# Tokens sorted by expert through DRAM: a mixture-of-experts stage moved from each batch to one pass over blocks of 128 slots at the end

## The reference

```python
xf = x.reshape(-1, Hd)
logits = xf @ Wg + bg
gates = jax.nn.softmax(logits, axis=-1)
idx = jnp.argmax(gates, axis=-1)
h = jax.nn.gelu(jnp.einsum('th,ehi->tei', xf, W1) + b1, approximate=False)
y = jnp.einsum('tei,eih->teh', h, W2) + b2
out = jnp.take_along_axis(y, idx[:, None, None], axis=1)[:, 0, :]
```

## Time and profile before

| | |
|---|---|
| time, median of 3 runs | 2138.87 us (2138.83 to 2142.31) |
| profiled execution, span | 2139.7 us |
| PE busy | 1961.1 us, 92% |
| DVE busy | 1713.5 us, 80% |
| ACT busy | 1318.5 us, 62% |
| POOL busy | 260.0 us, 12% |
| chain that ended last | PE 62%, DVE 27%, ACT 5%, DMA 3% |
| granted PE clock, 40 slices | 8 tenths in the first, 9 or more in the others |

### The profile page before, as it was taken

The page is one execution under the profiler, slowest core; times in us unless marked ns, Lnnn a source line. Parts: engine busy times, 40 slices in busy tenths (PEclk is TensorE's granted clock), DMA queues, the critical chain, the costliest instruction groups (busy, mean ns, idle before and its releaser), DMA issues.

```text
span 2139.7 us, 42900 instructions
## 1 busy us (share of the span) xinstructions
PE 1961.1 (92%) x17874; PEld 1108.8 (52%) x17874; DVE 1713.5 (80%) x2676; ACT 1318.5 (62%) x1957; POOL 260.0 (12%) x280
## 2 busy tenths in 40 slices
PE   4999988899999998889999998898999999889898
PEld 2677742424667773232566776333265777533235
DVE  8888878795878877699588887869878888786956
ACT  5666647386366655748546664565944666455682
POOL 1000001350000001035000000103500000011430
PEclk8999999999999999999999999999999999999999
DMA  6366700030055561012006665002001666300200
GB/s 275 75 127 129 142 32 13 10 113 11 21 103 129 126 120 34 6 32 91 11 21 126 126 127 124 12 2 102 22 11 44 133 123 130 94 13 9 94 2 11
DMA packets 424210, 156.39 MB, mean 73 GB/s; under 512 B 405928, under 2 KB 416560, under 8 KB 423120
## 3 DMA queue, kind: packets, MB, share of 16 engines
q1 hardware_dynamic: 423440, 151.54, 30.0%
q0 software_dynamic: 576, 2.10, 0.3%
HBM read 43.43 MB, written 2.16 MB: 21 GB/s over the span
## 4 chain that ended last, share of the span: by engine, by line
PE 62%; DVE 27%; ACT 5%; DMA 3%; issue 3%; POOL 0%; POOLq 0%; DVEq 0%; ACTq 0%; SPq 0%
DVE nmx L2052 14%; PE ps L655 11%; PE ps L657 11%; PE ps L656 11%; PE ps L1033 6%; PE ps L823 4%; PE ps L817 3%; PE ps L818 3%; PE ps L1019 3%; DMA arena<-arena 2%; PE ps L983 1%; DVE st L1691 1%; DVE arena L1862 1%; PE ps L1043 1%; PE ps L1100 1%
## 5 line engine op out<-in xcount | busy, mean ns | idle before, releaser
L2052 DVE TENSOR_REDUCE nmx<-ps 128x2 f32<-128x1024 f32 x384 | 444.7, 1218 | 15.2 <-PE ps L983 13.6
L1557 ACT ACTIVATE arena<-ps 128x512 f32<-128x512 f32 x768 | 406.3, 600 | 50.8 <-PE ps L1019 45.9
L655 PE MATMUL ps<-arena 128*128 128x512 f16 (+1 forms) x784 | 266.6, 340 | 1.3 <-DVE arena L1783 1.1
L657 PE MATMUL ps<-arena 128*128 128x512 f16 (+1 forms) x784 | 266.5, 340 | 0.0
L656 PE MATMUL ps<-arena 128*128 128x512 f16 (+1 forms) x784 | 266.5, 340 | 0.0
L1849 DVE TENSOR_SCALAR_CACHE_REDUCE ps<-ps 128x1536 f32<-128x1536 f32 x128 | 225.7, 1763 | 40.5 <-PE ps L657 39.8
L1033 PE MATMUL ps<-arena 128*17 128x256 f32 x3072 | 240.4, 389 | 0.0
L1862 DVE SCALAR_TENSOR_TENSOR arena<-arena,rs 128x1536 f16<-128x1536 f32 x128 | 231.6, 1810 | 4.2 <-ACT arena L1447 4.2
L1447 ACT ACTIVATE arena<-arena,rs 128x1536 f16<-128x1536 f32 x128 | 200.8, 1569 | 42.9 <-DVE rs L1855 42.9
L1440 ACT ACTIVATE arena<-ps,nm 128x1536 f32<-128x1536 f32 x128 | 197.1, 1540 | 10.3 <-DVE ps L1849 10.3
L817 PE MATMUL ps<-arena 128*128 128x128 f16 x1536 | 185.3, 219 | 1.6 <-DMA arena<-arena 1.6
(11 more groups left out here) (286 smaller groups left out, 3732.9 us busy)
## 6 DMA issues: line engine op xcount, KB each, us to landing
arena<-in_experts SPq DMA_DIRECT2D x4, 3840.0 KB, 11.5
arena<-in_weights SPq DMA_DIRECT2D x8, 929.0 KB, 19.1
arena<-arena SPq DMA_DIRECT2D x72, 64.0 KB, 2.1
arena<-in_ctx SPq DMA_DIRECT2D x4, 1024.0 KB, 5.3
arena<-arena SPq DMA_TRANSPOSE x256, 3.2
arena<-in_ctx_t SPq DMA_DIRECT2D x4, 1024.0 KB, 4.9
arena<-arena SPq DMA_DIRECT2D x72, 32.0 KB, 1.9
y<-in_x POOLq DMA_DIRECT2D x4, 512.0 KB, 4.2
```

Source lines behind the costliest of these rows:

```text
L655: mm(out_, lh, rh, start=(k == 0), stop=False)
L657: last = mm(out_, ll, rh, start=False, stop=(k == n - 1))
L1557: A(pr_[:, n % RING, :], ps[:, 4 + n % 3, :], ACT.Exp).then_inc(b_exp.sem, 1)
L2052: V.tensor_reduce(nmx[:, g_ % 2, ch, :, pp, i], ps[:, 2 * (z % 2):2 * (z % 2) + 2, :], AX.X, ALU.max, negate=True)\
```

## The change

The experts leave the batch loop. In every batch the normalised rows z (as fp16 halves, 512 values), the row of x after cross attention (256 values) and the token's number are collected in one SBUF tile `zx`, 520 words (2080 bytes) for each token. The logits are computed from DMA transposes of z, and the choice as before. A matmul with a triangular matrix of ones counts how many tokens before this one chose the same expert, and a running count `held` for each expert continues over the batches; together they give each token a slot. Expert e's slots begin at row e x 2432 of a DRAM tensor `zx_d`. Four indirect DMAs for each batch, 128 rows each, write the rows to their slots. In the last batch eight more DMAs write filler rows behind each expert's slots so far (7 x 640 and 896 rows, 11.2 MB).

At the end `block_tables` works out which 23 blocks of 128 slots exist (16 for 2048 tokens and at most 7 for experts' last blocks that are partly filled). The number of blocks is fixed at 23. For each block SP reads the block's row address into a register, loads z by a DMA transpose and x by a plain DMA into one of 6 buffers; PE reads the expert's address into a register and does 12 matmuls of 128 columns and 8 of 256 (the bias b2 comes in as two of them); ACT does two Gelus of 128 columns; DVE splits and adds; POOL scatters the 128 rows to the output by an indirect DMA, where filler slots have a row number beyond the bound and are skipped. The experts' weights are loaded and split once, in the last batch.

At a batch boundary `routed(b)` gives way to `next_window(b + 1)`, which does in a row what had been laid between the experts. `next_stats`, `next_moments` and `next_rows` move further forward, into cross attention; they read the next batch's x from a buffer of its own, `xn`, loaded by SP in the place of the experts' weights. The choice for batch b - 1 (`route_logits`, `route_choice`, `route_ranks`, `route_slots`) is done inside `windowed(b)`. ACT loads the Gelu table once, and the Exp table no longer at the start of `windowed`. The matmuls of `keep_warm` in `routed` are gone.

```diff
+            def keep_rows(b):
+
+                sp.wait_ge(lx_added.sem, lx_added.at(b, 2 * NT))
+                if b < B - 1:
+                    sp.wait_ge(b_mm.sem, b_mm.at(b, 192))
+                sp.dma_start(zx[:, :, D:2 * D], x[:]).then_inc(xc_in.sem, 16)
+
+            def transpose_rows(b):
+
+                sp.wait_ge(z_lo.sem, z_lo.at(b, 1))
+                for i in range(NT):
+                    sp.dma_start_transpose(zTt[b][:, 4 * i:4 * i + 4, :], z16[:, i, :]).then_inc(zt_in.sem, 16)
...
-                sp.dma_start(arena[:, HE:HE * 2 * NE], moe_in[:, 0:HE * (2 * NE - 1)]).then_inc(raw_in.sem, 16)
-                sp.dma_start(raw_last, moe_in[:, HE * (2 * NE - 1):HE * 2 * NE]).then_inc(raw_in.sem, 16)
+                if b < B - 1:
+                    sp.dma_start(xn, x_dram[bass.ds(b + 1, 1), :, 0:D].rearrange("b (i p) d -> p (b i) d", p=P)).then_inc(y_in.sem, 16)
...
-                sp.wait_ge(e_added.sem, e_added.at(b, NE))
-                sp.dma_start(out[bass.ds(b, 1)].rearrange("b (i p) d -> p (b i) d", p=P), x[:]).then_inc(x_out.sem, 16)
...
+                keep_rows(b)
+            transpose_rows(B - 1)
+            sp.wait_ge(zx_out.sem, zx_out.at(B, 16 * NE))
+            sp.wait_ge(e_table.sem, e_table.at(0, 1))
+            for j in range(NB):
+                r_ = j % BR
+                at = sp.value_load(where[0:1, 1, j:j + 1], min_val=0, max_val=NE * REGION - P)
+                if j >= BR:
+                    sp.wait_ge(e_h.sem, e_h.at(0, 2 * (j - BR)) + 2)
+                    sp.wait_ge(o_out[r_].sem, 16 * (j // BR))
+                rows = zx_d[bass.ds(at, P), :]
+                sp.dma_start_transpose(zb[r_], rows[:, 0:D].bitcast(F16)).then_inc(block_in[r_].sem, 16)
+                sp.dma_start(xb[r_], rows[:, D:ZW]).then_inc(block_in[r_].sem, 16)
...
+            def scatter_rows(b):
+
+                pool.wait_ge(r_slots.sem, r_slots.at(b, 1))
+                pool.wait_ge(z_lo.sem, z_lo.at(b, 1))
+                pool.wait_ge(xc_in.sem, xc_in.at(b, 16))
+                if b == B - 1:
+                    pool.wait_ge(zx_out.sem, zx_out.at(b, 16 * NE))
+                for i in range(NT):
+                    pool.indirect_dma_start(zx_d, bass.IndirectOffsetOnAxis(slot[:, i:i + 1], 0), zx[:, i, :], None)\
+                        .then_inc(zx_out.sem, 16)
...
+            def pad_regions():
+
+                for e in range(NE):
+                    n = PAD if e == NE - 1 else S + P
+                    at = pool.value_load(pad_at[0:1, e:e + 1], min_val=0, max_val=NE * REGION - n)
+                    pool.dma_start(zx_d[bass.ds(at, n), :], ident16_in.rearrange("a b -> (a b)").bitcast(F32)[0:ZW].unsqueeze(0).to_broadcast([n, ZW]))                        .then_inc(zx_out.sem, 16)
+
+            def scatter_block(j):
+
+                r_ = j % BR
+                pool.wait_ge(e_added.sem, e_added.at(0, j + 1))
+                pool.indirect_dma_start(out.rearrange("b s d -> (b s) d"), bass.IndirectOffsetOnAxis(row_at[:, r_:r_ + 1], 0), xb[r_][:, 0:D], None,
+                                        bounds_check=B * S - 1, oob_is_err=False).then_inc(o_out[r_].sem, 16)
...
+                        if b == B - 1:
+                            pad_regions()
...
+            def next_window(t):
+
+                transpose_context(t)
+                transpose_next(t)
+                pe.wait_ge(lx_added.sem, lx_added.at(t - 1, 2 * NT))
+                window_keys(t, range(4))
...
+            def route_logits(b):
+
+                pe.wait_ge(zt_in.sem, zt_in.at(b, 16 * NT))
+                for i in range(NT):
+                    last = product(ps[:, LOGIT_BANK, NE * i:NE * i + NE],
+                                   [((zTt[b][:, 4 * i + c, :], zTt[b][:, 4 * i + DC + c, :]), W("g", c, 0, NE)) for c in range(DC)])
+                last.then_inc(r_logits.sem, 1)
...
+            def block_hidden(j):
+
+                r_ = j % BR
+                at = pe.value_load(where[0:1, 0, j:j + 1], min_val=0, max_val=2 * (NE - 1) * EW)
+                pe.wait_ge(block_in[r_].sem, block_in[r_].at(0, 32 * (j // BR + 1)))
+                for m in range(DC):
+                    if j >= 2:
+                        pe.wait_ge(e_gelu.sem, e_gelu.at(0, 2 * (j - 2)) + m + 1)
+                    last = product(ps[:, HID_BANK[j % 2][m], 0:P],
+                                   [(tuple(ewc[:, bass.ds(at + (HE * part + D * c + P * m), P)] for part in range(2)),
+                                     (zb[r_][:, c, :], zb[r_][:, DC + c, :])) for c in range(DC)])
...
+                return at
+
+            def block_out(j, at):
+
+                pe.wait_ge(e_split.sem, e_split.at(0, j + 1))
+                if j == 0:
+                    pe.wait_ge(e_table.sem, e_table.at(0, 3))
+                if j >= 2:
+                    pe.wait_ge(e_added.sem, e_added.at(0, j - 1))
+                d_ = ps[:, OUT_BANK[j % 2], 0:D]
+                chosen = pick2[0:NE, j:j + 1].to_broadcast([NE, P])
+                mm(d_, chosen, b2h[:], start=True, stop=False)
+                mm(d_, chosen, b2l[:], start=False, stop=False)
+                for c in range(DC):
+                    hi, lo = (hgT[j % 2][part][:, c, :] for part in range(2))
+                    wh_, wl_ = (ewc[:, bass.ds(at + (2 * HE + HE * part + D * c), D)] for part in range(2))
+                    mm(d_, hi, wh_, start=False, stop=False)
+                    mm(d_, hi, wl_, start=False, stop=False)
+                    last = mm(d_, lo, wh_, start=False, stop=(c == DC - 1))
...
-                for e in range(NE):
-                    if 0 < e < NE - 1:
-                        expert_hidden(b, e + 1, (e + 1) % 2)
-                    if e == NE - 1 and b < B - 1:
-                        window_keys(b + 1, (0, 1))
-                        pe.wait_ge(e_gelu.sem, e_gelu.at(b, 2 * NE))
-                        window_keys(b + 1, (2, 3))
-                    expert_out(b, e, e % 2)
-                    if e == 3 and b < B - 1:
-                        transpose_next(b + 1)
...
+            def experts():
+                route_logits(B - 1)
+                route_ranks(B - 1)
+                pe.wait_ge(ew_lo.sem, 2 * NE)
+                pe.wait_ge(e_table.sem, e_table.at(0, 1))
+                at = [None] * NB
+                for j in range(NB + 1):
+                    if j < NB:
+                        at[j] = block_hidden(j)
+                    if j:
+                        block_out(j - 1, at[j - 1])
...
+            def rows_hi(b):
+
+                act.wait_ge(y_ready.sem, y_ready.at(b, Y_FIRST[6] + NT))
+                if b < B - 1:
+                    act.wait_ge(b_mm.sem, b_mm.at(b, 192))
+                A(z16[:, :, 0:D], zf, ACT.Copy).then_inc(z_hi.sem, 1)
+
+            def next_window(t):
+                context_affine(t)
+                next_hi(t)
+                rows_hi(t - 1)
+                window_hi(t)
+                context_hi(t)
...
+                if b:
+                    route_choice(b - 1)
...
+                if b:
+                    route_slots(b - 1)
...
                         context_moments(b + 1)
+                        next_stats(b + 1)
+                        next_moments(b + 1)
                         context_rows(b + 1)
+                        next_rows(b + 1)
...
+            def next_window(t):
+                normalise(t - 1, 4, x, zf)
+                next_lo(t)
+                window_lo(t)
+                rows_lo(t - 1)
+                for half in range(2):
+                    context_lo(t, half)
+
+            def rows_lo(b):
+
+                dve.wait_ge(z_hi.sem, z_hi.at(b, 1))
+                own.link(TS_(zx[:, :, 2 * D:ZW], token[:].unsqueeze(2).to_broadcast([P, NT, XW - D]), 1.0 * S * b, None, ALU.add))
+                TT(z16[:, :, D:2 * D], zf, z16[:, :, 0:D], ALU.subtract).then_inc(z_lo.sem, 1)
...
+            def route_slots(b):
+
+
+                dve.wait_ge(r_ranks.sem, r_ranks.at(b, 1))
+                own.link(TT(rank, ps[:, RANK_BANK, 0:NT * NE].rearrange("p (t e) -> p t e", t=NT), rows4(held[:]), ALU.add))
+                own.link(TT(rank, rank, lg[:, 4], ALU.mult))
+                own.link(V.tensor_reduce(slot_f, rank, AX.X, ALU.add))
+                own.link(TT(held[:], held[:], ps[:, RANK_BANK, NT * NE:NT * NE + NE], ALU.add))
+                if b == B - 2:
+                    own.link(V.tensor_copy(pad_at, held[0:1]))
+                V.tensor_copy(slot[:], slot_f).then_inc(r_slots.sem, 1)
...
+            def split_block(j):
+                dve.wait_ge(e_gelu.sem, e_gelu.at(0, 2 * j + 2))
+                if j >= 2:
+                    dve.wait_ge(e_y.sem, e_y.at(0, j - 1))
+                own.link(V.tensor_copy(hgT[j % 2][0], hg[:, j % 2]))
+                TT(hgT[j % 2][1], hg[:, j % 2], hgT[j % 2][0], ALU.subtract).then_inc(e_split.sem, 1)
+
+            def finish_block(j):
+                r_ = j % BR
```

(17 more changed lines are left out.)

319 lines of the change are left out of this document (166 added, 153 removed).

## The result

The kernel after takes 2153.35 us (median of 4 runs, 2148.68 to 2156.71), the kernel before 2139.45 (4 runs, 2138.83 to 2142.31). The ratio is 1.0067 with a 95% interval of 1.0048 to 1.0087: **slower by 0.7%**. The forecast was 2077, range 2055 to 2116, and so it was wrong by 76 us and in its sign. The profiled execution of the kernel after has a span of 2154.1 us, 14.4 more than before.

A forecast was written before the change was run, and what follows sets the result against it. PE's streaming was taken to bound the expert stage. 2139.7 - 108 (boundaries) + 41.8 (tail) + 2 (fillers) + 2 (clock) = 2077.5 us for the profiled execution; predicted median 2077, 8-in-10 range 2055 to 2116.

The forecast's parts named there:

- Boundaries: Three batch boundaries, last cross-attention addition to `add_rows`: 63.2 us falls to 26.2, taken as 36 saved each, 108 in all.
- Indirect DMA: POOL's scatters: 1.1 us each, bounds 0.84 and 2.5; four are free at a boundary up to 5.9 us.
- The rival of dear indirect DMAs: POOL's indirect DMAs at 3.1 us slow boundaries, blocks and ends by 36 us, giving 2113; chance 12%.
- the only slower outcome that I had priced: Indirect DMAs at 3.8 us or more eat the whole gain; at 4.5 us, 2166; chance 6%.
- Two small terms: Last batch's self attention: fillers cost 2 us, bounds 0 and 12; tail's first blocks: PE's low clock costs 2 us.
- late copies beside the fillers: Sign of being wrong: key copies landing late during the filler DMAs in the last batch's self attention; no size given.
- Tail: From the last addition to the end: 26.4 + 22 x 2.8 + 7.6 = 95.6 us, 41.8 more than before.
- Transposes for the logits: Tail's start: four DMA transposes at 0.75 us to issue and a landing of 2.4, done at +10.6.
- Blocks: Tail: 2.8 us a block, bounds 1.8 and 4.2, set by PE at 2.8, with SP at 2.1.
- the last block: Tail's end: hidden product, Gelu, split, output product, addition, scatter and landing, 7.6 us together.
- The register load: Each tail block: 0.8 us for loading an address into a register, between 0 and 1.9; no row showed it.
- Clock: Tail: PE waits some 12 us for the routing, so the first blocks run at 1.2 GHz, costing 2 us.

The follow-up runs named there:

- a_both: Kernel after with slot and token sharing one tensor, and smaller fillers written in the tail from SBUF on SP's queue: 2109.38 us, ratio 0.9856.
- a_512: Kernel after with its five new small SBUF tensors allocated behind the arena, which then starts at 130048 as before: 2128.38 us, ratio 0.9918 to 0.9956.
- best0: Kernel after with filler rows read from SBUF and the five new small tensors allocated behind the arena: 2079.01 us, ratio 0.9701 to 0.9728.
- best2: Against best0: ACT, not SP, loads blocks' x rows, five blocks ahead, into nine buffers; SP no longer waits for the output: 2071.76 us.

## Why the prediction was wrong, step by step

The span grew by 14.4 us where the sum had -62.2. The difference of 76.6 is: self attention with the fillers +49.6, latent attention +29.8, the tail with the clock's 2 us +2.7, boundaries -4.1, cross attention and the start -1.4.

- **Boundaries: right.** 108 us forecast, 112.1 measured (63.2 to 26.2 was forecast for each; from the end of the last addition it came to 25.4, 25.4 and 26.7). The statistics moved into cross attention cost nothing, as said: the stage is 0.6 us shorter in each batch.
- **Indirect DMA: right.** 1.1 us forecast, bounds 0.84 and 2.5. POOL, kernel after, before the last batch:

```profile
1534.67 1.80 POOL L679 DMA_INDIRECT zx_d<-arena,slot  x1 [24.70 <-DVE slot L2355]
1536.78 0.96 POOL L679 DMA_INDIRECT zx_d<-arena,slot  x1 [0.30 <-issue]
...
1540.28 0.74 POOL L722 TENSOR_TENSOR rstd<-ve,col 128x2 f32<-128x2 f32 x1
```

  From start to start it is 2.1 and then 1.26 us for each, the last 0.96 busy and 0.30 issue, so 5.6 for four where 5.9 were free. The 1/sqrt starts 6.0 us after `add_rows` (1534.29). `normalise` waits for POOL 3.2 us in 12 times over the whole kernel, exactly as before. The rival of dear indirect DMAs, and with it the only slower outcome that I had priced, did not come about. The Trainium skill, page "SBUF — State Buffer", section "A bandwidth-pool intuition that's wrong", had about 3100 ns for a GpSimd DMA beside a DVE copy; this trace does not show it: of the 23 scatters of the blocks 16 overlap such a copy, and all took 0.98 to 1.08 us.
- **"Two small terms": this is the step that failed.** "I take 2 us, bounds 0 and 12" for the fillers; it was 50 (self attention of the last batch 162.7 us, and 112.6 in a_both, which has no fillers there). I took the rate from the experts' load (3.84 MB in 11.5 us), a read of 3.84 MB of different addresses, and did not ask what this transfer reads: one row, again and again. At a third of the rate, 33 us of full DMA engines became 90, under a stage that cannot hide them, since PE needs four small copies one behind the other and each kept it waiting until 15 to 16 us after its issue. The bound of 12 went by the fast rate too. The prediction had named late copies beside the fillers as a sign of being wrong, and that is the sign that the profile shows.
- **A term that was missing: the arena's address, 30 us.** The forecast took the stages that the diff does not touch as unchanged. Their instructions were; their addresses were not. In the time it is 25 us (a_512), in the latent stages of the profiled executions 30.
- **Tail: 46.5 for 41.8, with the wrong engine.** Transposes for the logits: 1.29 us each to issue (5.17 for four) and not 0.75; they have landed at +12.2 and not +10.6, the first block starts at +27.8 and not +26.4. Blocks: 2.73 measured between scatters, 2.8 forecast. That these are so near is luck: SP's 2.63 and PE's 2.4 had been forecast as 2.1 and 2.8. What the sum had as the last block, 7.6, is 12.5: from the first block's start to its scatter 7.4 us, since PE does the second block's hidden product first and waits for its rows, and 5.1 from the last scatter to the end. The register load, the price that most of the doubt was said to lie in, took 0.28 to 0.30 us with 0.15 of register work behind it (0.8 forecast). The Trainium skill, page "DMA: Bandwidth & Descriptors", section "Latency and other measured facts", gives a floor of some 600 ns for a `tensor_load`; the trace's row is half of that, and doubling the load cost 0.56 us with all that belongs to it.
- **Clock: forecast 2 us, not measured by itself.** It did fall (0.54 over 2055 to 2080, 0.50 at the first block), and SP's first five steps, 2.57 to 2.59 us, were none the longer for it. It fell again at 2115, and SP's step of 4.35 us, 1.7 above its median, stands where the chain has run over PE at that clock and over a scatter's landing. How much of it is the clock's, no run shows.

With the fillers' source and the arena's place mended, and not a line of the sorting changed, best0 takes 2079.0 us for a forecast of 2077. Most of the sum for what the change does was sound, and it was lost to two things in how the kernel was written: a source row and a declaration's place. That it comes within 2 us is partly luck, for best0 gains 2 us more than forecast at the boundaries (110.2) and loses 4 more in the tail (45.5), and its step is right for the wrong engine. best2, at 2071.76, is the fastest of all the kernels, 3.15% faster than before (0.9671 to 0.9698). Of best0's span against before, some 4 us in the last batch's latent attention (214.3 for 210.1) remain unexplained.

## What to carry to other kernels

When a diff adds an on-chip tensor, ask what moves behind it: 32 bytes ahead of a buffer that DMA transposes read and write cost 1.1% here, with no instruction changed. Price a bulk transfer by what it reads as well as by its size, and ask which small latency-bound copies it shares the DMA engines with; "hidden" must be shown for those copies, not for the engines' average. In a stage of many small steps add up what each queue issues, register loads and DMA instructions too, before naming the engine that sets the pace; and a wait moved to another queue must be asked who stands behind it there.
